# Gated cross-attention with a 16-expert FP4 mixture: weight loads moved ahead in the DMA queue, and vector work dealt to other shared slots

## The reference

```
x = x + tanh(g_xattn) * (0.6*sigmoid(si + sj + b) + 0.4*layernorm(x))     # si, sj from ctx_512
h = layernorm(x)
probs = softmax(h @ gate_w.T);  top 4 of 16 experts, weights renormalised
act(h, e) = silu(h @ Wg[e]) * (h @ Wu[e]);   y(h, e) = act(h, e) @ Wd[e]
x = x + tanh(g_ffn) * (sum over the top 4 of w*y(h, e)  +  y(h, shared))
```

## Time and profile before

| | us |
|---|---|
| median of 3 runs | 690.98 |
| the three runs | 688.97, 691.63, 690.98 |
| the profiled execution, its own time | 689.59 |
| its span (first to last instruction) | 687.8 |
| PE busy, L1208 + L1222 + L1236 + L1192 and others | 622.2 (90% of the span) |
| DVE busy | 495.9 (72%) |
| ACT busy / POOL busy | 325.5 (47%) / 339.1 (49%) |
| mean granted PE clock | 0.982 |

### The profile page before, as it was taken

The page is one execution under the profiler, slowest core; times in us unless marked ns, Lnnn a source line. Parts: engine busy times, 40 slices in busy tenths (PEclk is TensorE's granted clock), DMA queues, the critical chain, the costliest instruction groups (busy, mean ns, idle before and its releaser), DMA issues.

```text
span 687.8 us, 17262 instructions
## 1 busy us (share of the span) xinstructions
PE 622.2 (90%) x4394; PEld 376.7 (55%) x4395; DVE 495.9 (72%) x1271; ACT 325.5 (47%) x558; POOL 339.1 (49%) x510
## 2 busy tenths in 40 slices
PE   3768869877898999999999999999999999999992
PEld 2444546445555566565655656565665656566561
DVE  6978788989676758687788767688588878767110
ACT  1763667331343454554445455454555544454541
POOL 2631844115234465555546555564655646565432
PEclk9999989998999999999999999999999999999997
DMA  8670111119156876758587684948767587644532
GB/s 233 220 228 2 62 46 63 48 41 286 51 156 146 201 172 141 170 126 184 111 210 164 143 210 82 227 74 202 175 136 175 118 202 160 148 89 78 91 38 41
DMA packets 49841, 93.72 MB, mean 136 GB/s; under 512 B 8840, under 2 KB 16776, under 8 KB 49816
## 3 DMA queue, kind: packets, MB, share of 16 engines
q0 software_dynamic: 16128, 38.35, 30.0%
q1 hardware_dynamic: 32936, 55.04, 27.4%
q10 hardware_dynamic: 752, 0.04, 0.1%
HBM read 65.16 MB, written 28.24 MB: 136 GB/s over the span
## 4 chain that ended last, share of the span: by engine, by line
PE 74%; DVE 10%; ACT 4%; DMA 4%; POOL 3%; issue 2%; SPq 1%; DVEq 0%; POOLq 0%; ACTq 0%
PE gu_ps L1208 43%; PE bank L1236 20%; PE bank L1248 4%; PE bank L1222 4%; DMA dn_sc<-dn_scale_halves 2%; DMA room_a<-in_ctx 1%; PE gu_ps L1168 1%; DVE act L995 1%; POOL mix_room L495 1%; ACT acth L626 1%; DVE X L1004 1%; DVE acth L1000 1%; PE bank L1165 1%; POOL room_a L461 1%; ACT mix_room L585 1%
## 5 line engine op out<-in xcount | busy, mean ns | idle before, releaser
L1208 PE MATMUL gu_ps<-wgu,mix_room 128*128 x1728 | 305.1, 326 | 3.4 <-DVE tick L954 2.1
L1208 PEld LDWEIGHTS gu_ps<-wgu,mix_room 128*128 128x128 f16 x1728 | 166.2, 98 | 115.1 <-issue 8.0
L1236 PE MATMUL bank<-wdn,aT 128*128 (+1 forms) x792 | 185.3, 379 | 4.2 <-ACT aT L633 3.7
L534 POOL DMA_INDIRECT out<-mix_room,idx_s x72 | 122.7, 1705 | 32.0 <-issue 30.9
L633 ACT ACTIVATE aT<-bank 128x768 f16<-128x768 f16 x88 | 71.2, 810 | 136.9 <-PE bank L1222 132.1
L1236 PEld LDWEIGHTS bank<-wdn,aT 128*128 128x128 f16 x792 | 77.3, 98 | 88.9 <-issue 2.2
L505 POOL TENSOR_TENSOR pool_tick<-ones 128x1 f32<-128x1 f32 x144 | 35.8, 249 | 163.4 <-DMA out<-mix_room,idx_s 86.4
L995 DVE SCALAR_TENSOR_TENSOR act<-gu_ps,wslot,sg x72 | 44.5, 617 | 96.4 <-ACT sg L619 84.4
L626 ACT ACTIVATE acth<-act 128x384 f16<-128x384 f32 x88 | 46.0, 523 | 128.2 <-DVE act L995 128.2
L516 POOL DMA_INDIRECT room_b<-token_rows,idx_g x72 | 76.9, 1067 | 12.2 <-issue 3.7
L1000 DVE TENSOR_TENSOR acth<-act,acth (+1 forms) x88 | 51.1, 580 | 38.2 <-ACT acth L626 37.8
(11 more groups left out here) (157 smaller groups left out, 594.6 us busy)
## 6 DMA issues: line engine op xcount, KB each, us to landing
dn_sc<-dn_scale_halves SPq DMA_DIRECT2D x34, 384.0 KB
dn_raw<-in_L_ffn_down_packed SPq DMA_DIRECT2D x48, 256.0 KB
gu_sc<-gu_scale_halves SPq DMA_DIRECT2D x34, 192.0 KB
X<-in_x SPq DMA_DIRECT2D x4, 1024.0 KB, 8.1
token_rows<-room_a SPq DMA_DIRECT2D x16, 256.0 KB, 2.0
out<-X SPq DMA_DIRECT2D x4, 1024.0 KB, 11.6
gu_raw<-in_L_ffn_gate_up_packed SPq DMA_DIRECT2D x16, 192.0 KB
gu_raw<-in_L_ffn_gate_up_packed SPq DMA_DIRECT2D x16, 191.9 KB
```

Source lines behind the costliest of these rows:

```text
L534: nc.gpsimd.indirect_dma_start(out[:, :], bass.IndirectOffsetOnAxis(idx_s[:, b:b + 1], 0), y_sb[:, b, :], None, compute_op=ALU.add).then_i ...
L1208: mm = nc.tensor.matmul(ps[b][:, 0:I], x(xp * HC + c), wgu[:, w, wp, c, col:col + I], start=(c == 0 and xp == 0 and wp == 0), stop=(c == H ...
L1236: mm = nc.tensor.matmul(y_ps[0 if shared else b][:, :], aT[:, b, ap, t, :], wdn[:, w, wp, t, :], start=(n == 0), stop=(n == 3 * IC - 1))
```

## The change

Six edits, on four queues.

1. SP: `load_expert` of n = 2 goes in between the eighth and the ninth store of token rows. `load_expert` of n = 3 goes ahead of the store of the routing weights and of the four output stores.
2. DVE: `first_weights(4)`, the last part of the first routed expert, goes from slot 15 to slot 9, ahead of `route()`. Parts 0 and 1 are both in slot 6 (before: slots 5 and 6). The next expert's first quarter (`dequant(2, 0, 0, None)`) stays in slot 15.
3. DVE: `x_factors(2)` goes to slot 2, `attend`/`second_stats` of batch 2 from slot 3 to slot 4, those of batch 3 from slot 4 to slot 5. The two clears of `r_keep` go from slot 6 to slot 3.
4. DVE, ahead of slot 2: three down quarters of the shared expert stand ahead of `activations(0)` instead of two. `attend(1)` and `second_stats(1)` stand ahead of `add_y(0)` and `take_words(1, 1)`. The `dq_ready` signal stands ahead of `activations(1)`.
5. POOL: `inverse_std` of batch 2 goes in between rows 5 and 6, and that of batch 3 behind batch 2's `scaled_x`. ACT: the sigmoids of batch 2 go ahead of the two `gwT` copies. DVE: `x_factors(0)` goes ahead of the split of the router weights.
6. DVE: `lnB` in one instruction instead of two (four times), and 72 instead of 68 `lead` clears at the start.

```diff
-        LEAD = 68
+        LEAD = 72
...
             for i in range(NT):

+                if i == 2 * TB:
+                    sp.wait_ge(dq_ready, 1)
+                    load_expert(sp, gu_packed[1], dn_packed[1], 0, 2)
...
+            sp.wait_ge(dq_ready, 2)
+            load_expert(sp, gu_packed[2], dn_packed[2], 1, 3)
             sp.wait_ge(cw_ready, 1)
...
-            sp.wait_ge(dq_ready, 1)
-            load_expert(sp, gu_packed[1], dn_packed[1], 0, 2)
             for b in range(B):
...
-            sp.wait_ge(dq_ready, 2)
-            load_expert(sp, gu_packed[2], dn_packed[2], 1, 3)
...
-            low_halves_x(1)
+            low_x(TB)
+            low_x(TB + 1)
             inverse_std(0, 2)
+            low_x(TB + 2)
+            low_x(TB + 3)
+            scaled_x(2)
             inverse_std(0, 3)
-            scaled_x(2)
             scaled_x(3)
...
             scores(1)
+            scores(2)
             for hl in range(2):
...
-            scores(2)
             scores(3)
...
-                step(nc.vector.tensor_tensor(lnB[:, at], lnA[:, at], mv[:, at, 0], ALU.mult))
-                step(nc.vector.tensor_scalar(lnB[:, at], lnB[:, at], -1.0, None, ALU.mult), wait=False)
+                step(nc.vector.scalar_tensor_tensor(lnB[:, at], mv[:, at, 0], -1.0, lnA[:, at], ALU.mult, ALU.mult))
...
                 if i == 2:
                     first_stats(2)
                     first_stats(3)
...
-                    attend(2)
-                    second_stats(2)
...
-                    first_weights(0)
...
                 if i == 9:
+                    first_weights(PARTS)
                     route()
...
                 if i == NT - 1:
-                    first_weights(PARTS)
...
-            take_words(1, 1)
             attend(1)
-            add_y(0)
             second_stats(1)
+            add_y(0)
+            take_words(1, 1)
```

More of the change, by code:

```diff
@@ L733, in norm_stats, with split_router @@
                                         ALU.add).then_inc(ve_ready[k], 1)
-            def split_gates():
+            def split_router():
                 step(nc.vector.tensor_scalar(gws[:, :], gws[:, :], R_SCALE, None, ALU.mult))
@@ L739, in split_gates, with scale_gates @@
                 nc.vector.tensor_tensor(gw_hl[:, 1, :], gws[:, :], gw_hl[:, 0, :], ALU.subtract).then_inc(gw_ready, 1)
+            def scale_gates():
                 v.wait_ge(tg_ready, 1)
@@ L974, in _ @@
             row_scores(0)
-            split_gates()
+            scale_gates()
             x_factors(0)
+            split_router()
             first_stats(1)
@@ L1016, in first_weights @@
                     end_dequant(1)
-                    dequant(2, 0, 0, None)
             def mark(j):
@@ L1038, in after_shared_slot @@
                     first_stats(3)
+                    x_factors(2)
                 if i == 3:
-                    x_factors(2)
                     x_factors(3)
+                    step(nc.vector.memset(r_keep[:, :, :], 1.0))
+                    step(nc.vector.memset(r_keep[:, :, 0:1], 0.0))
+                if i == 4:
                     attend(2)
                     second_stats(2)
-                if i == 4:
+                if i == 5:
                     attend(3)
                     second_stats(3)
-                if i == 5:
+                if i == 6:
                     first_weights(0)
-                if i == 6:
                     first_weights(1)
-                    step(nc.vector.memset(r_keep[:, :, :], 1.0))
-                    step(nc.vector.memset(r_keep[:, :, 0:1], 0.0))
                 if i in (7, 8):
@@ L1072, in after_shared_slot @@
                 if i == NT - 1:
-                    first_weights(PARTS)
-            for d in range(PARTS):
-                if d % 2 == 0:
-                    dequant(0, 0, None, d)
-                else:
-                    dequant(0, 0, None, d)
-                    activations(d // 2, d // 2, shared_w[:, 0:1])
-                    low_halves(d // 2, d // 2)
+                    dequant(2, 0, 0, None)
+            for d in range(PARTS - 1):
+                dequant(0, 0, None, d)
+            activations(0, 0, shared_w[:, 0:1])
+            low_halves(0, 0)
+            dequant(0, 0, None, PARTS - 1)
             v.wait_ge(dqs, 1 + PARTS * (G_STEPS + D_STEPS))
             nc.vector.memset(tick[:, 0:1], 0.0).then_inc(dq_ready, 1)
+            activations(1, 1, shared_w[:, 0:1])
+            low_halves(1, 1)
+            attend(1)
+            second_stats(1)
+            add_y(0)
             take_words(1, 1)
-            attend(1)
-            add_y(0)
-            second_stats(1)
             for i in range(2, NT):
```

## The result

The changed kernel takes **696.02 us** (median of 11 runs, 693.48 to 697.91) against 690.98 (11 runs, 688.55 to 694.15) for the kernel before: ratio 1.0071, 95% interval 1.0051 to 1.0091. Measured again beside other kernels it was 694.51 us, ratio 1.0051 (1.0034 to 1.0067). It is slower by 3.5 to 5 us. The forecast was 690.5 us and no change that can be told; its range ended at 694.5.

A forecast was written before the change was run, and what follows sets the result against it. PE was taken as the bound, busy 99.50 of 100 us from 224 us on, so only earlier idle and half-clock time counted. Terms summed to +0.25: 689.8 profiled, 691.2 on the median's scale, forecast 690.5 us, range 684.5 to 694.5.

The forecast's parts named there:

- front: Ahead of slot 2: earlier sigmoids and DVE reordering bring the fourth tile's rows to PE at 65.9, not 70.54: -4.65 us.
- batch 2: `attend(2)` behind `add_y(3)` gives most of the gain back; the eighth tile's rows reach PE at 90.8: +3.0 us.
- batch 3: `attend(3)` behind `add_y(4)` ends at 104.75, so `activations(6)` keeps nothing of the gain: +1.5 us.
- parts 0 and 4 ahead of `sel`: DVE between `activations(6)` and `sel` gains two weight parts and loses the clears, `sel` at 142.5: +4.75 us.
- clock at the count: PE's 3.8 us wait before the count may bring half-clock work behind it: +1.6 us, bounds 0 to 2.3.
- first routed slot: PE's 2.10 us wait before the first routed gate-up shrinks to 0.6: -1.6 us, bounds -0.9 to -2.1.
- load: Earlier load of n = 3 removes DVE's 4.17 us wait near 212, PE's idle and half-clock work: -4.35 us.
- rival 2: `activations(0)` and `(1)` come no earlier, rows 4 stay at 70.5, `attend(2)` still moves: 694.5 to 695.9 us; chance 0.10.
- PE's idle time in one piece: Before the eighth tile's rows near 91, PE idles some 9 us at once, before 2.52 and 2.92 in two.
- down(1)'s wait: PE's down(1) waits 2 us for `add_y(0)`, time it would otherwise spend waiting for the fourth tile's rows.
- the count's wait: PE waits from 138.7 for `sel` at 142.5, ahead of the count: 3.8 us in place of 1.30.
- The first (the collisions shrink): Half of DVE's 6 us waiting for POOL in weight parts 1 and 2 goes: 685.2 to 686.6 us; chance 0.24.

The follow-up runs named there:

- the front alone: Kernel before with only the ACT and DVE changes ahead of slot 2; loads, POOL's order and slots as before: 686.98 us, ratio 0.9946.
- alone -4.1: Kernel before with only the load of n = 3 moved ahead of the last output store: 685.82 us, ratio 0.9941.

## Why the prediction was wrong

Most mechanisms were those that it named; the sizes were off, nearly all to the same side. Predicted and measured, in us:

| term | predicted | measured | from |
|---|---|---|---|
| front | -4.65 | -3.7 | tile 4's rows on PE; the front alone |
| batch 2 | +3.0 | +3.5 | tile 8's rows on PE |
| batch 3 | +1.5 | +2.2 | `activations(6)` on DVE |
| parts 0 and 4 ahead of `sel` | +4.75 | +4.65 | from there to `sel` |
| clock at the count | +1.6 | +2.1 | gate-up and transposes |
| first routed slot | -1.6 | -0.64 | PE's wait 2.10, now 1.46 |
| load | -4.35 | -4.3, alone -4.1 | PE 8.11 late, then 3.80 |
| sum | +0.25 | +3.8 | |

The other 0.8 of the 4.63 us are in the routed part behind 324 us, most of it in the one wait for ACT shown above (0.81 for 0.21; 0.82 when the change ran again). The prediction had nothing there. Its cause was not tried and stays open.

**The step that failed** is the pair of paragraphs on the front and batch 2, with its continuation in batch 3: they said that nothing but 0.15 us of gain is left at `activations(6)`, and it was 1.99 of loss. That is 2.1 of the 4.4 us by which the sum missed; the first routed slot is 1.0, the routed part 0.8, the clock 0.5. Three things in the step:

- *"PE's first shared slot starts at about 43.4, just behind DVE's gate-up signal, which was given at 42.6."* I took 42.58 for a fixed time. In the change the signal came at 43.92, and PE waited 0.70 for it. The rows that the sum moved up did come up, by 2.24 for a forecast of 2.35 (ACT's first normalised row, before and with the change):

```profile
34.05 0.87 ACT L581 ACTIVATE room_a<-X,xm,xs 128x512 f16<-128x512 f32 x1
```

```profile
31.81 0.84 ACT L585 ACTIVATE room_a<-X,xm,xs 128x512 f16<-128x512 f32 x1
```

  PE, which had started 2.95 us behind the signal before, was held by it now and started 1.41 earlier in place of 2.1. Its first gate-ups then took 9.67 for 9.23. Over all profiles the signal varied: 41.04, 42.58, 43.44 and 43.88 with the old front, 43.34 to 44.61 (mean 43.73) in nine with the new one (one of them with the split in its old place). That the new front itself makes it 1.0 later, by rows of POOL's that now fall into the last quarters (which is the mechanism of rival 2, in part), fits: POOL's fourth row of batch 0 started at 40.81, ahead of the signal, where it had started at 43.02, behind it, and from the copy of its words to the signal DVE took 15.06 in place of 14.23. But with the old front that time was 13.29 to 14.98 in four profiles, with the new one 14.86 to 15.22 in nine, and four against nine don't settle it. A gate that sits 0.8 us ahead of a new start is the new bound as soon as it moves. On PE, the fourth tile's rows came 3.0 us earlier on average (66.64 to 67.42 with the new front, 68.74 to 70.61 with the old), and never the 4.65.
- *"From its end at 78.95: `add_y(3)` 0.6"* left out slot 4's own activations and low halves, which stand ahead of `add_y(3)` on DVE. The low half ran from 79.97 for 1.00 us beside POOL's `scaled_x(3)`, and `add_y(3)` began 1.0 behind the end of down(3). The mixing (2.72) and the statistics were as predicted. Of the 1.0, 0.4 came back behind `veps`: POOL's factors took less there, and the rows reached PE 4.9 us behind it in place of 5.3.
- *Batch 3's "0.9 for POOL's row work beside it"* was taken from the old order. There the mixing took 3.63, and 2.73 alone. In the new one two of POOL's low rows meet it, at 99.74 and 102.06:

```profile
99.74 1.38 POOL L462 TENSOR_TENSOR room_a<-mix_room,room_a 128x512 f16<-128x512 f32 x1 [5.29 <-ACT mix_room L589]
102.06 1.28 POOL L462 TENSOR_TENSOR room_a<-mix_room,room_a 128x512 f16<-128x512 f32 x1 [0.94 <-ACT mix_room L589]
```

and it took 4.53, 1.8 more than alone, some 0.9 for each. The Trainium skill (SBUF — State Buffer, "Who interferes with whom") says that a DVE instruction with two inputs in SBUF contends with a POOL instruction that reads SBUF. The rows agree, since both `attend` and the low half are of this kind. The sum had taken the collision of the old place for that of the new one.

What held: PE's idle time in one piece (9.27, "some 9 us"), down(1)'s wait of 1.88 for `add_y(0)` ("2 us"), the set of work to `sel` to 0.1, the count's wait (3.81, "3.8"), half clock behind it, and the load. The clock was 0.5 dearer than taken and inside its bounds, 0 to 2.3. The first routed slot gave 0.64, below the bound of 0.9: for what stays the profile names nothing that PE waited for (`issue`), and it measured 1.46 to 1.55 in all nine profiles in which part 4 came early. I had bounded it by 0.0 and 1.2, with no row to bound it by.

Of the rivals, none came true. The first (the collisions shrink) went the other way. The second (the front brings nothing) had nearly the right time, 694.5 to 695.9, by luck: most of the front's gain was there, and more of it than forecast was given back behind. The range ended 1.5 us under the median because it let each term err alone; five of them erred together. Each had been read from one execution; that this is why they erred to one side is likely, but not shown.

## What to carry to other kernels

Price a step that is moved behind another engine's result from the moment when that result is *used*, with everything that stands ahead of it in the queue, and look at which rows of the neighbour engine the new place falls on. A gain of one part of a change is worth what the other parts leave of it: run the parts alone and keep those that gain. Here that gave 0.9883 where the whole gave 1.0071 and 1.0051. Where a start is moved up to just behind another engine's signal, take the spread of that signal into the range.

## What the runs showed of the hardware

- The clock behind a wait is not a function of the wait. In the profiles with a wait of 3.3 us or more at the count (five, of four kernels) the gate-up behind it took 3.22 to 4.02 us every time. With a wait of 1.3 us it took 2.13 in seven profiles and 3.81 in one, and the same kernel's other profile is one of the seven. Behind the wait of 2.10 before the first routed gate-up it took 2.12 in three profiles and 3.47 in one. The last down matmuls of all stand behind a wait of 1.04 or 1.05 us in all thirteen profiles: they took 2.11 or 2.12 us in nine and 3.63 to 3.80 in four. The Trainium skill (TensorE: Matmul & The Clock Gate, "What's actually happening") says that the number of slow matmuls at the start of a kernel varies between its runs; the pair shows the same in the middle of one, with 1.7 us. A profile in which the clock stays up is no proof that it will.
- A short DVE operation of 0.56 us with two inputs in SBUF took 1.00 beside POOL's scaling, and a mixing of 2.73 took 4.53 beside two POOL rows of 1.3. Such operations are cheap or dear by where they fall.
- A queue in order carries a delay to work that has nothing to do with it: POOL's wait of 3.56 us for batch 3's factors held back batch 2. One line of DVE's order took that wait away; `activations(6)` came 2.19 us earlier on DVE and the time fell by 2.9 us (1 to 5 by the intervals).
